# A fused attention and feed-forward kernel: its loop over pairs written out, eight raw buffers for one stage, and a prologue in another order

## The reference, cut to what matters

```python
x = L0_attn_x                         # (4, 2048, 512), float32
xn = _layernorm(x)                    # over the last axis
shifted = pad(xn, one token)[:, :-1]
xr, xk, xv = (mu * xn + (1 - mu) * shifted for each of mu_r, mu_k, mu_v)
r, k, v = xr @ Wr.T, xk @ Wk.T, xv @ Wv.T          # 512 x 512 each
wkv = wkv_v4(k, v, w, u)              # a recurrence over the 2048 tokens
attn = (sigmoid(r) * wkv) @ Wo.T
hidden = silu(xn @ W1.T) * (xn @ W3.T)             # W1, W3: 2048 x 512
ffn = fwht(hidden) @ W2.T             # Hadamard transform over 2048, W2: 512 x 2048
return x + attn + ffn
```

## Time and profile before

| what | value |
|---|---|
| median of 3 runs | 2781.82 us (2778.17 to 2783.24) |
| profiled execution | 2782.27 us, span 2780.5 us |
| TensorE busy | 2673.2 us (96%), 11584 matmuls |
| VectorE, ScalarE, GpSimd busy | 2201.4, 1316.3, 230.0 us |
| DMA | 699.33 MB, mean 252 GB/s |

### The profile page before, as it was taken

The page is one execution under the profiler, slowest core; times in us unless marked ns, Lnnn a source line. Parts: engine busy times, 40 slices in busy tenths (PEclk is TensorE's granted clock), DMA queues, the critical chain, the costliest instruction groups (busy, mean ns, idle before and its releaser), DMA issues.

```text
span 2780.5 us, 37363 instructions
## 1 busy us (share of the span) xinstructions
PE 2673.2 (96%) x11584; PEld 2180.0 (78%) x11584; DVE 2201.4 (79%) x2954; ACT 1316.3 (47%) x2107; POOL 230.0 (8%) x180
## 2 busy tenths in 40 slices
PE   5887889999999999999999999999999999999998
PEld 3566668888888888888888888888888888888887
DVE  4688997688887888878886888868888688877784
ACT  4654445444463445544454434644446444554442
POOL 1176760000000000000000000000000000000000
PEclk9999999999999999999999999999999999999999
DMA  9667668687786878778786877868777786876777
GB/s 299 262 246 241 222 241 286 225 270 244 252 277 232 274 218 277 249 253 260 238 269 225 281 241 251 274 226 271 237 265 263 240 270 218 275 247 223 227 231 261
DMA packets 247575, 699.33 MB, mean 252 GB/s; under 512 B 33200, under 2 KB 33328, under 8 KB 246832
## 3 DMA queue, kind: packets, MB, share of 16 engines
q1 hardware_dynamic: 247344, 696.56, 75.7%
HBM read 583.15 MB, written 113.31 MB: 250 GB/s over the span
## 4 chain that ended last, share of the span: by engine, by line
PE 82%; DVE 3%; issue 2%; ACT 1%; DMA 0%; POOL 0%; ACTq 0%; DVEq 0%
PE gamma L825 11%; PE gamma L828 11%; PE gamma L827 11%; PE acc L835 10%; PE acc L837 10%; PE acc L836 10%; PE gamma L907 4%; PE gamma L909 4%; PE gamma L908 4%; PE alpha L825 2%; PE alpha L828 2%; PE alpha L827 2%; PE alpha L909 1%; PE alpha L908 1%; PE alpha L907 1%
## 5 line engine op out<-in xcount | busy, mean ns | idle before, releaser
L1000 ACT ACTIVATE step<-gamma 128x512 f32<-128x512 f32 x512 | 305.9, 597 | 842.0 <-PE gamma L828 805.5
L825 PE MATMUL gamma<-xs_high,wring 128*128 128x512 f32 x1280 | 503.8, 394 | 43.1 <-POOL wring L703 18.1
L828 PE MATMUL gamma<-xs_low,wring 128*128 128x512 f32 x1280 | 501.2, 392 | 0.0
L827 PE MATMUL gamma<-xs_high,wring 128*128 128x512 f32 x1280 | 501.1, 392 | 0.0
L835 PE MATMUL acc<-vring,hid 128*128 128x512 f32 x1232 | 481.2, 391 | 12.0 <-POOL vring L703 5.9
L836 PE MATMUL acc<-vring,hid 128*128 128x512 f32 x1232 | 479.6, 389 | 0.0
L837 PE MATMUL acc<-vring,hid 128*128 128x512 f32 x1232 | 479.4, 389 | 0.0
L825 PEld LDWEIGHTS gamma<-xs_high,wring 128*128 128x128 f32 x1280 | 241.7, 189 | 103.3 <-issue 20.9
L835 PEld LDWEIGHTS acc<-vring,hid 128*128 128x128 f32 x1232 | 231.6, 188 | 65.8 <-issue 13.3
L828 PEld LDWEIGHTS gamma<-xs_low,wring 128*128 128x128 f32 x1280 | 242.0, 189 | 51.1
L1283 DVE SCALAR_TENSOR_TENSOR step<-xt,vec,step 128x512 f32<-128x512 f32 x192 | 144.3, 755 | 172.8 <-ACT step L969 172.2
(11 more groups left out here) (113 smaller groups left out, 4685.9 us busy)
## 6 DMA issues: line engine op xcount, KB each, us to landing
wring<-u_split SPq DMA_DIRECT2D x336, 512.0 KB, 4.1
vring<-d_split SPq DMA_DIRECT2D x288, 512.0 KB, 4.2
wring<-r_split SPq DMA_DIRECT2D x180, 512.0 KB, 4.2
raw<-spilled SPq DMA_DIRECT2D x160, 256.0 KB, 4.2
spilled<-step SPq DMA_DIRECT2D x128, 256.0 KB, 4.2
wlast<-u_split SPq DMA_DIRECT2D x112, 256.0 KB, 3.2
u_split<-wring SPq DMA_DIRECT2D x48, 512.0 KB, 3.0
res<-x SPq DMA_DIRECT2D x16, 1024.0 KB, 7.7
```

The costliest lines, as they stand in the source:

```text
L825: pe.matmul(bank[:, :], w[:, 0, col], high, start=fresh and kt == 0, stop=False, skip_group_check=True)
L827: pe.matmul(bank[:, :], w[:, 1, col], high, start=False, stop=False, skip_group_check=True)
L828: last = pe.matmul(bank[:, :], w[:, 0, col], low, start=False, stop=kt == 1, skip_group_check=True)
L1000: act.activation(to, bank[:, :], ACT.Copy).then_inc(u_copied, 1)
```

## The change

1. `over_pairs` writes out all eight pairs; the loop and its registers go.
2. `raw` has 8 slots: four more lie in the four tiles of `res`. The first 54 raw units go round all eight, the other 10 round the first four. The first load of the residual into `res` moves from step 7 to step 14 of pair 0 and waits for the splits that read those slots.
3. The prologue: r units 0 to 8 run first, then the pass within tiles, r units 9 to 14, the pass across tiles, r units 15 to 23. SP loads the raw units and x rows before W2, and W2 in four pieces among the first r steps; the statistics of half b are computed in VectorE's steps 0 to 2; stages 0 and 1 of the first recurrence item stand at step 8, stages 3 to 6 in front of step 9, stage 7 at step 12. The half-turned tiles are loaded with the last quarter first, and its final store has a semaphore of its own (`tail_stored`). The `xs` work moves to steps 15 to 23.

```diff
-RAW = 4
+RAW = 8
+RAWS_IN_RES = 54
+RAW_SLOT = [m % RAW if m < RAWS_IN_RES else m % 4 for m in range(len(RAWS))]
...
+PASS_ONE_AFTER, PASS_TWO_AFTER = 8, 14
+TURN_ORDER = [W2_LOADS - 1] + list(range(W2_LOADS - 1))
...
-FIRST_MADE_AT = {n: n - 13 for n in range(13, 17)}
-FIRST_HIGH_AT = {n: n - 13 for n in range(13, 20)}
-FIRST_LOW_AT = {n: n - 17 for n in range(17, 24)}
+FIRST_MADE_AT = {16: (0, 1), 17: (2,), 18: (3,)}
+FIRST_HIGH_AT = {15: (0,), 16: (1,), 17: (2, 3), 18: (4,), 19: (5,), 20: (6,)}
+FIRST_LOW_AT = {18: (0,), 19: (1,), 20: (2,), 21: (3,), 22: (4, 5), 23: (6,)}
...
+        raw += [res[:, i, :] for i in range(RAW - 4)]
...
         def over_pairs(eng, pair):
-            pair(0)
-            with eng.Fori(1, PAIRS - 1) as s:
+            for s in range(PAIRS):
                 pair(s)
-            pair(PAIRS - 1)
...
-                if j == 7:
+                if j == (14 if is_first(s) else 7):
                     load_residual(s, 0)
...
             def first_down_step(n):
-                if n < 12:
+                if n < PASS_ONE_AFTER:
                     store_split(("r", n))
                 if n == 1:
+                    load_w2(0)
+                if n == 2:
+                    load_columns_first(1)
+                if n == 3:
+                    load_w2(1)
+                    store_tokens(0, 1)
+                if n == 4:
                     load_tokens(0, 1)
-                if n < W2_LOADS:
-                    store_half_turned(n)
-                if W2_LOADS < n <= 2 * W2_LOADS:
-                    load_half_turned(n - W2_LOADS - 1)
-                if n == 11:
+                    load_w2(2)
+                if n == 5:
+                    load_w2(3)
+                if n == PASS_ONE_AFTER:
+                    for i in range(PASS_ONE_AFTER, 12):
+                        store_split(("r", i))
                     for i in range(W2_LOADS):
-                        store_turned(i)
+                        store_half_turned(i)
                 if 12 <= n + 3 < R_UNITS:
                     load_r(0, n + 3)
+                if 0 <= n - PASS_ONE_AFTER - 1 < W2_LOADS:
+                    load_half_turned(TURN_ORDER[n - PASS_ONE_AFTER - 1])
+                if n == PASS_TWO_AFTER:
+                    for i in TURN_ORDER:
+                        store_turned(i)
...
-            for n in range(12):
-                r_unit(0, n)
-            turn_across_tiles()
-            for n in range(12, R_UNITS):
-                r_unit(0, n)
+            for n in range(R_UNITS):
+                r_unit(0, n)
+                if n == PASS_ONE_AFTER:
+                    turn_within_tiles()
+                if n == PASS_TWO_AFTER:
+                    turn_across_tiles()
...
-                if h == 0 and pair == 1:
+                if h == 0 and pair == 1 and not (isinstance(r, int) and r == 0):
                     wait(dve, tok_stored, r, 32)
```

More of the change, by code:

```diff
@@ L79, with held_before @@
 RAW_AT = {u: n for n, u in enumerate(RAWS)}
-RAW = 4
+RAW = 8
+RAWS_IN_RES = 54
+RAW_SLOT = [m % RAW if m < RAWS_IN_RES else m % 4 for m in range(len(RAWS))]
+RAW_TURN = [RAW_SLOT[:m].count(slot) for m, slot in enumerate(RAW_SLOT)]
+def held_before(m):
+    earlier = [k for k in range(m) if RAW_SLOT[k] == RAW_SLOT[m]]
+    return RAWS[earlier[-1]] if earlier else None
 def freed_by(raw):
@@ L155, in build @@
         xt = sb("xt", [P, KT, 2 * N + 1])
-        raw = [sb(f"raw{i}", [P, C]) for i in range(RAW)]
+        raw = [sb(f"raw{i}", [P, C])[:, :] for i in range(4)]
         hidb = [raw[i] for i in range(HIDB)]
@@ L578, in store_split @@
                 sp.dma_start(to, split_place(unit).bitcast(f32)).then_inc(stored_in(unit)[0], 16)
-                while raws[0] < len(RAWS) and freed_by(RAWS[raws[0] - RAW]) <= n:
+                reach = RAW_AT["d", 1] if unit[0] == "r" else len(RAWS)
+                while raws[0] < reach and freed_by(held_before(raws[0])) <= n:
                     load_raw(raws[0])
@@ L1512, in down_step @@
                 r = s + 1
+                if not with_d and n == PASS_ONE_AFTER + 1:
+                    for stage in range(3, 7):
+                        wkv(r, 0, stage)
+                if not with_d and n in (1, 2):
+                    dve.wait_ge(stats_made, 4 + 2 * n)
+                    token_mean_var(1, n - 1)
+                if not with_d and n < 2:
+                    token_stats(0, 1, n)
+                if not with_d and n == 2:
+                    add_eps(0, 1)
                 if with_r:
```

184 lines of the change are left out of this document (99 added, 85 removed).

## The result

The changed kernel takes **2762.97 us** (median of 4 runs, 2761.43 to 2763.72); the kernel before took 2779.99 us beside it (4 runs, 2777.4 to 2783.24). The ratio is 0.9937, 95% interval 0.9922 to 0.9952: 17 us faster. The prediction said 2742, 40 us faster. The measured time lies inside the predicted range, but less than half of the gain came.

What follows compares the result with a forecast made beforehand. TensorE, busy 96% of the span, was taken as the bound, so only its idle time could be won: 2782.3 - 9 - 17 - 14 = 2742.3, less 0.45, gave 2742 us, range 2722 to 2764.

Steps and rivals of the forecast that it cites:

- Part 1: Pair loop: writing it out removes five back edges, 1.87 us each in the trace; 9 us won, bounds 5.2 to 9.4.
- the cost of nothing for instruction loading: Written-out loop: a longer program was costed at nothing, since pairs 0 and 7 were written out already.
- Part 2: Prologue: first r unit at 22.6 us, 93.5 of work, 15 of waits; first up product at 131, 17 us won.
- (a): Prologue: a `wring` slot is split again only after its old unit's `r_split` store lands; 6 us of waits.
- Rival 3: Slower: flight of an `r_split` store decides, losing if it reaches about 23 us; 2799 at 27 us; chance 0.05.
- (b): Prologue, ScalarE: pass one's 16 copies stand behind the split of r 11, which waits for r 8's store; 5 us.
- (c): Prologue: evacuations of the four banks and DVE's seven xs steps at the end; 4 us of waits.
- counted at nothing: Prologue: statistics for half 1, moved among DVE's r steps, cost nothing; some 3 us if that cover is gone.
- Part 3: First up stage: eight raw buffers remove POOL's waits for w1 and w3; 14 us won, bounds 0 to 23.
- POOL is free when the buffer is: First up stage: reason given for taking 14 us, nearer the 18.1 us of TensorE's waits for `wring`.
- rival 2: First up stage: DVE is the bound and buffers move the wait to its gate steps; 2755 us; chance 0.14.
- the prediction's signs of being wrong: ScalarE waiting at `wring` splits, `r_split` over 12 us in flight; up stage DVE over 95% busy, TensorE waiting for it.

Runs made afterwards that it cites:

- experiment 1: Changed kernel with pairs 1 to 6 put back in a loop, everything else kept: 2774.86 us, ratio 0.9981.
- experiment 3: Changed kernel with the second token rows' load moved behind the store of r 5, centring and scaling of half b one step later: 2763.26 us.
- experiment 4: experiment 3 with the third and fourth W2 loads also moved, behind the stores of r 6 and r 7: 2755.06 us, ratio 0.9911.
- experiment 2: Changed kernel with four raw buffers again and the residual loaded at step 7 of pair 0: 2769.69 us, ratio 0.9963.
- experiment 5: Changed kernel (eight raw buffers) with the reciprocal of recurrence items 1 to 6 of the first pair replaced by a multiplication: 2756.38 us.
- experiment 6: The four-raw-buffer kernel of experiment 2 with the same reciprocals replaced as in experiment 5: 2762.66 us, ratio 0.9934.
- experiment 10: Changed kernel with POOL's four sums of w1 and w3 cut to 32 of 256 columns in steps 1 to 15 of the first pair: 2750.45 us.
- experiment 7: experiment 4 with raws 2 and 3 loaded ahead of the first token load, second token load and both W2 loads later, centring a step later: 2759.60 us.
- experiment 8: experiment 7 with ScalarE's rectified and exponential steps of the first recurrence moved behind copies 6 and 12 of pass one: 2762.33 us.
- experiment 9: experiment 4 with r 11's split and the exponents later among pass one's copies, first products waiting only for xs steps they read: 2753.29 us.
- experiment 12: experiment 11 with five 256 KB raw loads moved behind the store of r 8: 2751.45 us, ratio 0.9898.
- experiment 11: experiment 9 with stages 3 to 6 of the first recurrence spread over steps 9 to 11, each behind that step's mix: 2753.89 us.

## Why the prediction was right and wrong

**Part 1, the loop (9 us): right.** The periods give 7.9, the loop put back costs 10 to 12 (experiment 1). The step that took 1.87 us an edge from the trace held. The 0.108 us that the Trainium skill gives for a compare-and-branch ("Advanced Engine Details and Errata", Control Flow Timing) would make five edges worth 0.5 us, if the instruction's own time were all that an edge costs; experiment 1 has some 2 us an edge, so it is not. In the program written out TensorE's waits from 430 to 2700 us come to 3.9 us in all, and the period of the pairs fell to 327.3; the cost of nothing for instruction loading stands.

**Part 2, the prologue (17 us): this step failed; it gave 3.5.** The start was given as 22.6, bound 27.6, and came at 25.2: DVE began to centre at 18.67 where 17 was taken, and from there to the first r unit it took 6.6 us where 5.6 was counted (the steps that the prediction lists add up to 5.3, not 5.6). The work of 93.5 us was right; the 353 matmuls read for the old prologue are 355, which changes nothing. The waits were put at 15 us and were 25.9 (144.6 - 25.2 - 93.5), just above the bound of 25. By their terms:

- (a), the stores of `r_split`, taken as 6 us, was 13.2: the wait of 10.7 at r 8, and 2.5 because r 8 then ran at 0.43 us a matmul instead of 0.228, the 1.2 GHz level, right behind that wait. The condition was right (three units, 8.2 us, for flight and splits). I then spread 13.5 MB evenly over the stretch and did not ask where in SP's order they lie. At one place they stood together: the token row's store, for which SP stops some 4 us, then 1 MB, then the store of r 5. Rival 3 had this mechanism and dismissed it for want of 7 MB ahead of a store. Far fewer were needed, as ScalarE's order passes the delay on to the evacuation, r 9 and TensorE. Experiments 3 and 4 show that moving the token load alone gave nothing, and moving the two W2 loads as well 7.3 us. The sentence from the Trainium skill ("DMA: Bandwidth & Descriptors", Queues, rings and completion order), that a ring is taken in its order, had put all of (a) on bytes ahead. These runs agree in part: without a W2 load just ahead of it the store of r 5 was in flight for at most 6.3 us instead of 10.2, and the other 4.6 us are a late issue.
- (b), the split of r 11 ahead of pass one, was taken as 5. Pass one lasted 15.9 us instead of 13.3, so 2.6 were lost, but by another cause: the split of r 11 did not wait in the changed kernel. Ahead of the exponents, among the copies, ScalarE waited for DVE's `z`, and TensorE then waited 1.98 us for the next copy (the row at 77.01 above). Of that recurrence the prediction weighed only stages 3 to 6, and `z` is made in stage 1. ScalarE's timeline:

```profile
74.38 1.06 ACT L1074 ACTIVATE e<-z 128x1024 f32<-128x1024 f32 x1 [2.15 <-DVE z L1389]
```

With r 8 earlier, in experiment 4, the wait of (b) did come, 2.48 us and slower issues behind it, of 5.2 lost in all.

- (c) was taken as 4 and was 4.9: 2.7 for the xs steps, 1.5 and 0.7 at evacuations.
- Not foreseen: 2.5 us because the first r unit also runs at 0.43 us a matmul, after 25 us of idling; and 2.0 us at r 4. There the statistics for half 1, "counted at nothing", lost their cover on an engine that the step did not look at. POOL's inverse root for half 1 stands ahead of the low part of r 4 and waits for DVE's statistics; its timeline in the changed kernel:

```profile
38.08 1.01 POOL L727 TENSOR_TENSOR mean_rstd<-var_eps,half 128x4 f32<-128x4 f32 x1 [3.78 <-DVE var_eps L1286]
39.06 2.82 POOL L733 TENSOR_TENSOR wring<-res,wring 128x512 fp32r<-128x512 f32 x2
```

- Of the rest, 0.6 us is a wait for a load from `r_split` at r 14.

**Part 3, the buffers (14 us): right in kind, too large; they gave 7 to 8** (experiment 2). POOL's wait for `sums` went, as said, and TensorE's for `wring` fell from 18.1 to 4.8 us. But TensorE's wait for DVE's gate step rose from 9.0 us (5 times) in the kernel before to 20.6 (7 times): 11.6 of the 13.3 us came back. The failed sentence is that POOL is free when the buffer is: it looked only at one wait. DVE, POOL and TensorE are all behind in this stage, and a shorter wait for one is followed by one for another. That is rival 2's mechanism in part; rival 2 itself, which says that the gain is nearly nil, was too strong. Experiments 5, 6 and 10 show that no engine alone is the bound: 14 us less of DVE gives 4.5 (7.3 with four buffers), and 41 us less of POOL gives 11.6, with some 14 us less of DVE. What holds the stage at 245 us even then, against 205 at full speed, stays open, as does how POOL's effect divides between its own lateness and DVE's slower instructions.

Of the prediction's signs of being wrong, the waits were there: ScalarE with no engine named at the split into `wring`, and TensorE for DVE steps. The sizes named with them were not: `r_split` was in flight for a median of 8.3 us from 20 to 60 us and not over 12, and one store, r 5's at 10.2 us or less, was enough; DVE was busy 89% of the window of the up stage and not over 95%.

## What to carry to other kernels

When a step is moved ahead in a queue, follow one instance of its slowest resource through every engine's program: which issue stands ahead of the store, what stands behind the instruction that waits for it, and who waits for that. A mean rate says nothing about one store that decides. A small store for which the whole queue waits should have nothing large right behind it (experiment 7), and loads that are not read soon belong behind the stores on which a ring turns (experiment 4). An experiment that moves one instruction out of the way puts it in the way of another: read what the moved one delays (experiments 7 to 9). Of a wait that will go, count as gain only what the next-latest engine leaves of it: in this stage, with POOL busy 72%, TensorE 85% and DVE 89%, about half was left.

## What the runs showed of the hardware that was not expected

- The lower clock costs in two places: r 0 after 25 us without work and r 8 after 10.5 us both took 5.3 us for 12 matmuls instead of 2.7. In experiments 4 and 12, where the wait at r 8 was 3.1 and 1.7 us, r 8 took 2.84 us, and the granted clock of 50 to 100 us was 0.97 and 1.00 instead of 0.86. But after waits of 2.5 and 3.0 us in experiments 9 and 11 it took 4.4 and 5.3 us: the length of the last wait does not decide it, and what does is not shown here.
- DVE's gate steps with two SBUF inputs take 1.4 to 1.5 times as long in the stage in which POOL is busy as in a steady pair (0.95 to 1.01 us against 0.68 to 0.69), and those with an input in PSUM take the same in both (0.69). With 41 us less of POOL (experiment 10) only part of this went, and other things also differ between the stages.
- A 4 KB store to DRAM let the next load be issued 4.5 to 5.3 us after it in eleven traces, and 5.6 and 5.9 us after it in the two with 512 KB of loads issued right behind the store.
